# A row gather's wait on its ring place: ScalarE's copy of the turned tile in place of TensorE's transpose

## What is computed

```python
xn = _layernorm(x, axis=-1)
s = _L0_attn_ref(xn, ...)                     # relu(rope(xn @ W_Q)), tanh, group norm, transpose
idx, w = _route(xf, Wr, br)                   # 6 of 32 experts for each row
h = jnp.square(jax.nn.relu(xf @ w1.T)) @ w2.T # one expert
acc = acc + g[:, None] * h                    # summed over the experts by their gates
shared = jnp.square(jax.nn.relu(hidden_tensor @ Ws1.T)) @ Ws2.T
x = x + s * silu(shared + acc)
```

## Time and profile before

| what | before |
|---|---|
| median of 3 runs | 384.15 us (383.17 to 384.49) |
| span of the profiled execution | 381.1 us |
| PE busy | 308.8 us, 81% of the span |
| DVE busy | 269.4 us, 71% |
| ACT busy | 240.6 us, 63% |
| POOL busy | 221.0 us, 58% |
| gathers of rows (L607) | 91, busy 93.7 us |
| first and last gather of rows start at | 91.6 us and 247.9 us |
| first and last transpose of a slot tile start at | 105.5 us and 256.4 us |

### The profile page before, as it was taken

One profiled execution on the slowest core, in us unless ns is written; L12 is line 12 of the kernel. 1 busy time (PEld: TensorE's weight loads), 2 busy tenths in 40 slices (PEclk: granted clock), 3 DMA queues, 4 the chain that ended last, 5 costly groups with the idle time before them and its releaser, 6 DMA issues.

```text
span 381.1 us, 8188 instructions
## 1 busy us (share of the span) xinstructions
PE 308.8 (81%) x2716; PEld 234.7 (62%) x2716; DVE 269.4 (71%) x634; ACT 240.6 (63%) x383; POOL 221.0 (58%) x232
## 2 busy tenths in 40 slices
PE   0585886899996878789798888789797798799962
PEld 0353654667785757677575676676475477687841
DVE  4688889998955286647567564447855786699866
ACT  5878799555484676676686576796645653544432
POOL 1966889855877356454663646500076565666750
PEclk9998699899999899999999999999999899899997
DMA  7951160254773366364644646434597565567742
GB/s 262 400 177 58 21 214 24 87 169 137 241 253 101 95 171 206 113 193 126 193 140 132 205 131 211 143 113 136 180 320 223 151 181 150 174 168 207 204 110 83
DMA packets 38762, 62.89 MB, mean 165 GB/s; under 512 B 5026, under 2 KB 26690, under 8 KB 38722
## 3 DMA queue, kind: packets, MB, share of 16 engines
q1 hardware_dynamic: 31474, 42.57, 34.4%
q0 software_dynamic: 7248, 19.80, 18.2%
HBM read 46.66 MB, written 15.70 MB: 164 GB/s over the span
## 4 chain that ended last, share of the span: by engine, by line
PE 52%; DVE 16%; issue 9%; ACT 9%; DVEq 6%; another core or an unknown queue 3%; POOL 2%; ACTq 2%; DMA 1%
PE hp L947 5%; PE hp L945 4%; PE hp L946 4%; PE rot L909 4%; PE hp L932 4%; PE dp L1001 4%; PE dp L1004 4%; PE dp L1003 4%; DVE xs L1284 3%; DVEq L1286 3%; PE hp L934 3%; PE bp L892 3%; DVE hf L1260 2%; PE rot L960 2%
## 5 line engine op out<-in xcount | busy, mean ns | idle before, releaser
L607 POOL DMA_INDIRECT xgt<-xtab,ids x91 | 93.7, 1029 | 63.7 <-PE rot L909 36.3
L617 POOL DMA_INDIRECT wst<-ytab,slot x60 | 62.7, 1045 | 61.3 <-DMA ytab<-wst 27.1
L688 ACT ACTIVATE hf<-hf 128x512 f32<-128x512 f32 (+1 forms) x80 | 49.9, 623 | 72.1 <-DVE hf L1260 52.8
L1001 PE MATMUL dp<-wt,hhi 128*128 128x256 f16 x204 | 56.7, 278 | 5.2 <-ACT xs L722 2.9
L1277 DVE COPY wst<-rot 128x512 f32<-128x512 f32 (+1 forms) x35 | 23.7, 680 | 51.7 <-PE rot L962 37.9
L1004 PE MATMUL dp<-wt,hhi 128*128 128x256 f16 x204 | 56.6, 277 | 1.2 <-issue 1.2
L1003 PE MATMUL dp<-wt,hlo 128*128 128x256 f16 x204 | 56.6, 278 | 1.0 <-issue 1.0
L693 ACT ACTIVATE hhi<-hf 128x512 f16<-128x512 f32 (+1 forms) x80 | 49.9, 624 | 5.7
L945 PE MATMUL hp<-xh,wt 128*128 128x512 f16 (+1 forms) x148 | 51.1, 345 | 0.9 <-DVE hf L1260 0.6
L703 ACT ACTIVATE xgt<-rot 128x1024 f16<-128x1024 f16 (+1 forms) x46 | 46.1, 1002 | 7.8 <-remote 5.0
L947 PE MATMUL hp<-xh,wt 128*128 128x512 f16 (+1 forms) x148 | 50.9, 344 | 0.0
(11 more groups left out here) (174 smaller groups left out, 703.1 us busy)
## 6 DMA issues: line engine op xcount, KB each, us to landing
gate_bc<-gtab SPq DMA_DIRECT2D x48, 256.0 KB
ytab<-wst SPq DMA_DIRECT2D x45, 256.0 KB
wst<-in_wts SPq DMA_DIRECT2D x17, 512.0 KB, 5.6
xs<-in_x SPq DMA_DIRECT2D x4, 512.0 KB, 5.0
xgt<-in_x SPq DMA_DIRECT2D x4, 512.0 KB
out<-xgt SPq DMA_DIRECT2D x16, 128.0 KB
xtab<-xn SPq DMA_DIRECT2D x3, 512.0 KB, 3.1
xgt<-xtab,ids POOLq DMA_INDIRECT x91
```

Of the source, the lines that this page charges most:

```text
L607: nc.gpsimd.indirect_dma_start(xg[:, a % XRING, :, :].rearrange("p h d -> p (h d)"), None, xtab, bass.IndirectOffsetOnAxis(ids[:, a:a + 1] ...
L617: nc.gpsimd.indirect_dma_start(yk[:, n % KRING, :], None, ytab, bass.IndirectOffsetOnAxis(slot[:, n // K, n % K:n % K + 1], 0))\
L688: nc.scalar.activation(hf[:, k % HP, 0:width(k)], hf[:, k % HP, 0:width(k)], ACT.Square, scale=W_SCALE ** (-0.5 if gated else -1.0))
L1001: nc.tensor.matmul(o, hhi[:, k % HRING, hcols], hi, start=(e == 0 and q % 2 == 0), stop=False, skip_group_check=True)
```

## The change

The gather for slot tile a waits for the count of copied tiles (raised by ACT, by two for each pair) instead of the count of turned tiles (raised by PE, by one for each tile). The number that it waits for is unchanged. Nothing else is touched: both counts are still raised and still used elsewhere.

```diff
             for a in range(TILES):
                 if a >= XRING:
-                    pool.wait_ge(t_done, a - XRING + 1)
+                    pool.wait_ge(xt_copied, a - XRING + 1)
                 nc.gpsimd.indirect_dma_start(xg[:, a % XRING, :, :].rearrange("p h d -> p (h d)"), None, xtab,
```

## The result

The changed kernel takes 399.63 us (median of 4 runs, 398.45 to 402.29). The kernel before took 383.66 us beside it (4 runs, 382.04 to 384.49). The ratio is 1.0437 (95% interval 1.0393 to 1.0481). The direction was forecast, the size was not: the change costs 16.0 us where some 3 were expected, and the time is outside of the range of 383.5 to 390.0. The profiled execution has a span of 398.3 us against 381.1.

The account below looks back on a forecast made before the run. TensorE was taken to bound the kernel. The median of 384.15 us plus a 3.0 us stall, with nothing for the steady part, gave 387.15, stated as 387.0 us since idle time may swallow a little; range 383.5 to 390.0 us.

Parts of the forecast that it names:

- What bounds: TensorE's in-order queue: a delay at 115 us makes the whole program late unless it falls into idle time.
- The release of gather 8: First ring reuse on POOL: gather 8 starts 0.27 us behind ACT's copy, at 110.86, which is 4.75 us later.
- Four gathers at 1.25 us: Gathers 8 to 11 on POOL follow at 1.25 us each, so gather 11 starts at 114.61 at the earliest.
- The landing: From a gather's start until TensorE can turn its tile: at most 3.94 us, read from tile 11.
- the far end of 6.03 us: Longest landing considered, read from the first result gather, which uses another table under heavy DMA load.
- The stall: TensorE waits ahead of tile 11 at the first ring reuse: 1.1 to 4.7 us, taken as 3.0 us.
- No second stall: Tiles 12 to 15: gather 15 lands by 123.55, before its turn at 124.4, because the first stall makes room.
- The steady part at nothing: Later tiles: tightest is tile 83, with 4.2 us left against a landing of at most 3.94; costed at nothing.
- rival 2: Starvation all along with 6 us landings: first stall 5.2 us, steady part 3.3 us, 392.6 us; chance 0.08.
- Rival 3, the clock: Idle TensorE brings one more half-clock period, 0.7 to 1.3 us on top of the stall; 388 to 389 us; chance 0.12.
- Rivals 1 and 4: Stall absorbed in idle time, 384.2 to 385.2 us, chance 0.18; earlier weight load makes it faster, 383.3 us, chance 0.07.

Follow-up runs that it names:

- e2: Kernel before with only gathers 8 to 15 waiting for ACT's copy count, later ones for PE's turn count; ratio 1.0087 at the 350 us level.
- e2b: Kernel before with only gathers 8 to 15 waiting for ACT's copy count, run again at the 384 us level; ratio 1.0107.
- a0: The whole change, unaltered, run again beside the kernel before at the 350 us level; ratio 1.0211.
- e7: Kernel before with gathers 8 to 15 waiting for the copy, plus filler matmuls in TensorE's waits for tiles 10 and 11; ratio 1.0128 at 350 us.
- e8: Changed kernel with ten gather ring places in place of eight and six turned-tile places in place of eight; 397.55 us, ratio 1.0402.
- b0: Kernel before, unchanged, profiled once more for its trace at the 350 us level; 351.77 us.
- e11: Changed kernel with four small POOL operations, about 1.3 us together, ahead of every fourth gather; 444.40 us, ratio 1.1533.
- e1: Kernel before with only gathers from 16 on waiting for ACT's copy count, 8 to 15 for PE's turn count; ratio 1.0104 at 350 us.

## Why the prediction was wrong, point by point

**What bounds.** Right: TensorE was the engine whose delay counts. That its wait for late tiles would end up in the time was borne out by e2 and e2b, which are slower by 3.0 and 4.1 us with both intervals above 1.

**The release of gather 8.** Right to 0.01 us: 0.26 us behind the copy, against 0.27.

**Four gathers at 1.25 us.** Right: gathers 8 to 11 span 3.75 us (112.17 to 115.92).

**The landing.** For the first stall the bound of 3.94 us held and was 0.6 to 0.8 us too long: 118.01 - 114.67 = 3.34 us for tile 10 and 119.10 - 115.92 = 3.18 us for tile 11, up to the turn. The Trainium skill ("DMA: Bandwidth & Descriptors", "Anatomy of one DMA — SWDGE (gpsimd) path") gives, as an estimate, 2.3 us; the measurement is 0.9 to 1.0 us longer, and it decides. But 3.94 us was read from one gather, that of tile 11, and taken as a bound for all. At the 350 level turns waited for landings of 4.3 to 6.3 us (a0, tiles 14, 27, 80 and 82), so the far end of 6.03 us, set aside as that of a result gather, is within what a row gather takes.

**The stall.** Taken at 3.0 us, measured 1.86 us as idle time, and 3.0 us (at 350) and 4.1 us (at 384) as time of the kernel in e2 and e2b. The sum of this part came out right in part by luck: the landing was taken too long, and the lower clock and the gaps behind the stall, which make tile 12 late by 6.1 us and not 1.9 in the kernel after, were taken as nothing.

**No second stall.** Wrong at the 350 level: e7 waits again at tile 15, a0 at tile 14. The forecast let the first stall make room; POOL keeps its pace of 1.25 us per gather, which is no faster than TensorE takes the tiles of a group once it is at full clock.

**The steady part at nothing.** This is the step that failed, in two ways. The margin (4.2 us against a landing of 3.94) was read from a trace of the 384 level and held to one landing. At 350 TensorE comes for its tiles sooner: for tiles 81 to 83 it leaves 5.5 to 5.9 us from gather to turn in the kernel before and 4.0 to 4.8 us in the changed one, and 3.6 us are lost. That is rival 2's mechanism, starvation all along, with landings of 3.9 to 6.3 us from tile 14 on, and its 3.3 us for the steady part is near that; its first stall of 5.2 us is not what was measured. At the 384 level, where the forecast was made, landings cost nothing in the steady part, as it said (tile 83 was turned 7.0 us after its gather in the kernel after, not 4.2, since the turn came later as well), and the steady part costs 15.5 us all the same, by a way that was not in the sum.

**Rival 3, the clock.** The mechanism was named and mis-sized. It allowed one more period of 2.5 us at half clock, worth 0.7 to 1.3 us. The first one alone lasts from about 119 to 129 us, with L1001 at 0.42 in place of 0.27 us, and in all there are 27.4 us more, spread over the steady part and not only behind the stall. What stood in the rows and was not followed up: gaps of 1.11 and 1.19 us with no named wait, right ahead of the slow matmuls. They were read as room that might swallow a stall, when gaps like them stand right ahead of most of the stretches at the lower clock.

**Rivals 1 and 4.** The stall was not absorbed: 1.0087 and 1.0107, both intervals above 1. Nothing got faster in the window from 105 to 115 us; DMA's share went from 0.72 to 0.73.

**What stays open.** Why ACT's count costs 4% at the 384 level when PE's count, later by a pair, costs nothing: by its rhythm, as some of the traces suggest and e8 does not, or by something else that follows ACT. What puts TensorE's instructions 0.7 us apart behind a row of gathers, and what makes the same kernel run at 350 us or at 384 us. It isn't TensorE's waits for landings or the offset loads, each of which was taken away. Whether the loading of the program has a part wasn't tested; the profile counts the same 24 packets in its instruction queue q8 at both levels, before and after the change. A filler that keeps the clock was tried at 350 us only, so how much of the 15.5 us is the clock and how much the gaps themselves is open too. None of the kernels beats the one before with all of its work done.

## What to carry to other kernels

A wait that is moved to a later counter also changes the rhythm of what it releases: read how many instructions each step of the new counter lets go and how long the pause behind them is, and not only whether each is still early enough. (That the rhythm is what cost 4% here isn't shown; that equal or greater lateness on the old counter cost nothing is.) If the bound engine already has gaps without a named wait and slow instructions behind them, give the slow instructions a term of their own: here the gaps hardly grew, and the time at half clock went from 6.8 to 34.2 us. A margin read from one trace holds for that trace's pace, and a landing read from one gather for that gather; where the margin is as thin as 0.3 us, price the stall.

## What the runs showed of the hardware

- The same kernel takes 350 or 384 us, at different times on one chip. At 384 us TensorE has 19.5 us of idle time with no named wait between 100 and 290 us (before), at 350 us only 1.0 us (b0).
- A row gather of 128 rows of 1 KB holds POOL for 0.95 us when undisturbed (1.02 us in the mean), and the next follows 0.30 us later. Where TensorE waited for the data, it began to turn them 3.2 to 3.3 us after the start of the gather in the kernel after, 3.1 to 6.3 us in a0, and 2.7 us (e11) to 6.5 us (e1) over all traces.
- TensorE's granted clock fell behind waits for landings, for DVE and behind gaps with no named wait alike. Two waits of 1.16 and 0.70 us were followed by 10 us at half clock in the kernel after.
- Filling 1.9 us of TensorE's waits with matmuls kept the granted clock at 1.00 in place of 0.83 over 10 us, and the kernel was no faster for it (1.0128 against 1.0087 of the kernel before): the engine met the next late tile.
